# Batched attention on one core: a third bank for exponentiated scores, short uses in the ring of maxima banks, and outputs that keep the heads on partitions

## The reference, cut to what matters

```python
x = x + attn_a(_layernorm(x), w_qkv, w_proj)          # causal, 16 heads of 16, T = 512
x = x + ffn(_layernorm(x), ...)                       # full attention, then a routed expert layer
x = x + attn_b(_layernorm(x), ...)                    # short attention with relative positions
x = x + ffn(_layernorm(x), ...)                       # the same weights as the second layer

# attn_a, per head                                    # ffn's attention, per head
a = where(causal, q @ k.T * 0.25, -inf)               # scores = q @ k.T * 0.25
a = clip(a, -100, 100)                                # probs = softmax(scores)
e = exp(a - max(a))                                   # attn = probs @ v, then @ Wo + bo
p = e / (sum(e) + 1e-6) + 1e-8
out = (p / sum(p)) @ v, then @ w_proj.T
```

## Time and profile before

| | |
|---|---|
| runs of the kernel before | 2593.06, 2582.32, 2595.44 us; median 2593.06 us |
| the profiled execution | 2579.53 us, span of its instructions 2577.8 us, mean granted PE clock 0.977 |
| PE busy | 2418.6 us, 94% |
| DVE busy | 1831.9 us, 71% |
| ACT busy | 1438.2 us, 56% |
| POOL busy | 1351.5 us, 52% |
| DMA | 305.88 MB, mean 119 GB/s |

### The profile page before, as it was taken

How to read it: one execution, slowest core, us unless ns; L and a number is a source line. 1 busy time by engine, 2 the same in 40 slices (tenths; PEclk the granted TensorE clock), 3 DMA queues, 4 the chain that set the end, 5 groups by cost and what they waited for, 6 DMA issues and landing times. The chain is left out here.

```text
span 2577.8 us, 45874 instructions
## 1 busy us (share of the span) xinstructions
PE 2418.6 (94%) x14724; PEld 1393.9 (54%) x14724; DVE 1831.9 (71%) x3685; ACT 1438.2 (56%) x2991; POOL 1351.5 (52%) x1358
## 2 busy tenths in 40 slices
PE   6999999999999999989999699988999999989998
PEld 3455555554444444349899366653344434349997
DVE  5999999999778888854333558867778888845333
ACT  3666666666777777753333232214777777653332
POOL 5356666563234554444655579843334454435655
PEclk8999999999999999999999799988999999999999
DMA  5333333333434444324665200015434444335654
GB/s 161 101 105 107 105 102 108 112 105 96 120 112 124 133 129 125 98 93 161 213 201 179 72 1 17 17 58 138 118 109 129 129 130 122 85 118 176 202 194 141
DMA packets 249936, 305.88 MB, mean 119 GB/s; under 512 B 28034, under 2 KB 224865, under 8 KB 249700
## 3 DMA queue, kind: packets, MB, share of 16 engines
q1 hardware_dynamic: 238164, 275.37, 35.8%
q0 software_dynamic: 10176, 26.27, 2.9%
q10 hardware_dynamic: 1360, 1.31, 0.2%
HBM read 210.32 MB, written 92.84 MB: 118 GB/s over the span
## 5 line engine op out<-in xcount | busy, mean ns | idle before, releaser
L783 DVE TENSOR_REDUCE neg_max_af<-sc_af 128x1 f32<-128x512 f32 (+3 forms) x864 | 551.0, 664 | 105.2 <-PE sc_af L489 101.2
L704 ACT ACTIVATE prob_af<-sct_af 128x512 f32<-128x512 f32 (+1 forms) x864 | 484.1, 582 | 234.9 <-PE sct_af L512 231.3
L783 DVE TENSOR_REDUCE neg_max_f<-sc_f 128x1 f32<-128x512 f32 x512 | 334.6, 685 | 93.0 <-PE sc_f L489 90.8
L704 ACT ACTIVATE prob_f<-sct_f 128x512 f32<-128x512 f32 x512 | 290.6, 598 | 127.5 <-PE sct_f L512 126.1
L512 PE MATMUL sct_af<-stack_q_af,stack_k_af 99*128 99x512 bf16 (+3 forms) x1024 | 320.1, 343 | 7.9 <-ACT prob_af L704 7.1
L489 PE MATMUL sc_af<-stack_k_af,stack_q_af 96*128 96x512 bf16 (+3 forms) x1024 | 320.0, 342 | 4.1 <-DVE neg_max_af L783 4.0
L1620 PE MATMUL y_ps_e<-w_r,hT_e 128*128 x1120 | 255.4, 381 | 5.7 <-issue 4.0
L812 DVE SCALAR_TENSOR_TENSOR prob_af<-prob_af,w_r 128x512 f32<-128x512 f32 (+2 forms) x224 | 233.2, 1049 | 21.7 <-ACT prob_af L704 21.5
L1807 DVE TENSOR_TENSOR y_e<-y_ps_e,b_e 128x256 f32<-128x256 f32 x70 | 29.7, 425 | 298.3 <-PE y_ps_e L1620 296.5
L540 PE MATMUL out_af<-prob_af,v_aug_af 128*32 128x512 f32 (+3 forms) x2048 | 231.9, 525 | 8.7 <-DVE prob_af L812 7.8
L1620 PEld LDWEIGHTS y_ps_e<-w_r,hT_e 128*128 128x128 f32 x1120 | 207.2, 190 | 35.3 <-issue 9.4
(11 more groups left out here) (383 smaller groups left out, 4650.0 us busy)
## 6 DMA issues: line engine op xcount, KB each, us to landing
w_r<-in_f_W_dram SPq DMA_DIRECT2D x66, 1024.0 KB, 5.1
stack_k_af<-k_parts_d SPq DMA_DIRECT2D x64, 384.0 KB, 4.3
k_parts_d<-parts_af SPq DMA_DIRECT2D x187, 128.0 KB
q_parts_d<-parts_af SPq DMA_DIRECT2D x96, 128.0 KB
stack_q_af<-q_parts_d SPq DMA_DIRECT2D x64, 192.0 KB, 2.9
stack_k_f<-k_parts_d SPq DMA_DIRECT2D x32, 384.0 KB, 4.2
w_next<-in_f_W_dram SPq DMA_DIRECT2D x12, 1024.0 KB, 4.9
k_parts_d<-parts_f SPq DMA_DIRECT2D x91, 128.0 KB
```

The costliest lines, as they stand in the source:

```text
L704: nc.scalar.activation(dst, src.rearrange("p (h q) -> p h q", h=len(heads)), ACT.Exp).then_inc(S.exp_done, 1)
L783: nc.vector.tensor_reduce(M.neg_max[:, qt, heads[0]:heads[-1] + 1], src, AX.X, ALU.max, negate=True).then_inc(S.max_done, 1)
```

## The change

- PSUM: three `sct` banks (`exp` may lag three units), three `sc` banks, one `out`, one `gen`. The light uses now take turns with the scores in the ring of the three `sc` banks (`place`, `used_before`); heavy uses have `gen`.
- Outputs keep the heads on partitions. SP moves the 16 rows of each head from `o_sb` straight into `attT`, which is double now, and the row sums into `sums` (`move_out`, 5 DMAs a group). For each half of the heads (a chunk, c = 0 or 1) DVE works out the weights on a [128, 32] tile (`weigh`: 4 instructions causal, 1 otherwise), SP stores them to DRAM (`store_weights`) and reads them back repeated over each head's 16 rows (`spread_weights`), and POOL multiplies `attT` by them in place (`scale_out`: 3 instructions causal, 1 otherwise). The transposes `out` and `attT`, `normalise`, `add_floor` and ACT's copy of `attT` go.
- The old way stays for the second chunk of the last two units of each call that ends in ffn units (`by_pe`: n = 14, 15, 22, 23).
- The three bf16 parts of the maxima are laid out so that one transpose of [128, 48] does for four of [128, 12]; `max_sb` is [48, 128] instead of [12, 512].
- The sum of all v comes as one column per chunk (two matmuls of 1 column) instead of 256 columns on all partitions.
- Some pairs of semaphores are merged.

```diff
-    closing = [("out", last, NG - 1), ("attT", last, 0), ("attT", last, 1), ("y", last, 0), ("y", last, 1)]
-    for at, use in enumerate(opening):
-        place(use, (at + 1) % 2)
+    closing = [("out", last, NG - 1), ("attT", last, 1), ("y", last, 0), ("y", last, 1)]
...
+    def bank(use):
+        uses, at = place_of[use]
+        return M.sc[at % len(M.sc)] if uses is ring else M.gen
+
+    def used_before(use):
+        uses, at = place_of[use]
+        back = len(M.sc) if uses is ring else 1
+        return uses[at - back] if at >= back else None
     for n in range(first, end):
         for s in range(SLOTS_N):
-            if light_at(n, s):
-                place(light_at(n, s), 1)
-            if heavy_at(n, s) and s % 2 == 0:
-                place(heavy_at(n, s), 0)
+            g, kt = divmod(s, KT)
+            light, heavy = light_at(n, s), heavy_at(n, s)
+            for i in range(4):
+                place_scores(*group(n, g + 2), kt, i)
+                if light and i == (2 if kt == KT - 1 else 0):
+                    place(light, ring)
+            if heavy and s % 2 == 0:
+                place(heavy, gen_uses)
...
+            def move_out(n, g):
+                if not exists(n) or by_pe(n, g // 2):
+                    return
+                c, h = divmod(g, 2)
+                sp.wait_ge(S.o_sb, NG * n + g + 1)
+                if n > 1:
+                    sp.wait_ge(S.y_ps, 2 * (n - 1))
+                if exists(n - 1) and by_pe(n - 1, 1):
+                    sp.wait_ge(S.attT_ps, pe_chunks(n - 1))
+                sp.dma_start(M.sums[64 * h:64 * h + 64, :], M.o_sb[HD:P:32, :]).then_inc(S.moved, 16)
+                for i in range(4):
+                    o = 64 * h + HD * i
+                    sp.dma_start(M.attT[n % 2][o:o + HD, c, :], M.o_sb[32 * i:32 * i + HD, :]).then_inc(S.moved, 16)
+
+            def store_weights(n, c):
...
+                sp.wait_ge(S.weighed, chunks(n, c))
+                sp.dma_start(M.weights_d[n % NB][0, hs, :], M.weights[:, 0, :]).then_inc(S.weights_stored, 16)
+                if causal(n):
+                    sp.dma_start(M.weights_d[n % NB][1, hs, :], M.weights[:, 1, :]).then_inc(S.weights_stored, 16)
+
+            def spread_weights(n, c):
...
+                sp.wait_ge(S.weights_stored, 16 * spreads(n, c))
+                sp.wait_ge(S.moved, 80 * moved(n, 2 * c + 1))
...
+                for at in range(2 if causal(n) else 1):
+                    sp.dma_start(M.spread[:, at, :], M.weights_d[n % NB][at, hs, :].unsqueeze(1).to_broadcast([8, HD, T])).then_inc(S.weights_spread, 16)
...
-                    for t in range(KT):
-                        last = nc.tensor.transpose(Gb[0:12, t * P:t * P + P], M.max_parts[:, t, :, :].rearrange("p a h -> p (a h)"), C.ident_bf[:, :])
+                    last = nc.tensor.transpose(bank(use)[:, :].bitcast(BF16)[0:12 * KT, 0:P], M.max_parts[:, :, :, :].rearrange("p a h t -> p (a h t)"),
+                                               C.ident_bf[:, :])
...
                 u = exp_unit(n, g, kt, i)
-                if u >= 2:
-                    pe.wait_ge(S.exp_done, u - 1)
-                bank = M.sct[u % 2]
+                if u >= 3:
+                    pe.wait_ge(S.exp_done, u - 2)
+                bank = M.sct[u % 3]
...
             def read_out(n, g):
                 act.wait_ge(S.pv_done, pv_count(n, g, KT - 1))
-                if n > 0 or g > 0:
-                    act.wait_ge(S.out_ps, NG * n + g)
+                pn, pg = group(n, g - 1)
+                if exists(pn) and by_pe(pn, pg // 2):
+                    act.wait_ge(S.out_ps, outs(pn, pg))
+                elif exists(pn):
+                    act.wait_ge(S.moved, 80 * moved(pn, pg))
...
+            def weigh(n, c):
...
+                dve.wait_ge(S.moved, 80 * moved(n, 2 * c + 1))
...
+                    nc.vector.tensor_scalar(M.e8[:, :], M.sums[:, :], 1e-6, 1e-8, ALU.add, ALU.mult).then_inc(S.norm_step, 1)
...
+                    nc.vector.tensor_tensor(M.weights[:, 1, :], M.e8[:, :], M.weights[:, 0, :], ALU.mult).then_inc(S.weighed, 1)
...
                         if kt == 2:
                             normalise(pn, pg)
+                        if kt == 3 and pg % 2 == 1:
+                            weigh(pn, pg // 2)
...
+            def scale_out(n, c):
...
+                pool.wait_ge(S.weights_spread, 16 * spreads(n, c))
+                out = M.attT[n % 2][:, c, :]
+                if causal(n):
...
+                    nc.gpsimd.tensor_tensor(out, out, M.spread[:, 0, :], ALU.mult).then_inc(S.floor_v, 1)
+                    nc.gpsimd.tensor_scalar(M.spread[:, 1, :], M.spread[:, 1, :], M.v_all[:, n % 2, c:c + 1], None, ALU.mult).then_inc(S.floor_v, 1)
...
+                    nc.gpsimd.tensor_tensor(out, out, M.spread[:, 1, :], ALU.add).then_inc(S.attT_ready, 1)
```

301 lines of the change are left out of this document (168 added, 133 removed).

## The result

The changed kernel takes 2659.43 us (median of 4 runs, 2643.36 to 2674.43), the kernel before, measured beside it, 2590.18: the ratio is 1.0265, with a 95% interval of 1.0237 to 1.0294. It is slower by 2.6%; the forecast was 2533 us, faster by 2.3%. The profiled span is 2641.6 us against 2577.8, the mean granted PE clock 0.954 against 0.977.

The account below looks back on a forecast made before the run. PE was taken as the bound, nearly full in causal and full in ffn units; -73 (PE's list) + 8 (ring) + 13 (maxima rows) - 7 (third bank) - 1 (tail) = -60 us from 2593: 2533 us, range 2500 to 2572.

Parts of the forecast that it names:

- all five cases: PE's list decides (0.58), costs hide too (0.15), DVE holds causal units (0.12), transfers run late (0.07), no effect (0.08).
- the slow one: SP's list: maxima rows of every causal group leave late, 31 floor rows each stand 2.9 us more; 2610 us, chance 0.07.
- the first case: PE's shorter list in the attention units decides the time: 2533 us, bounds 2510 to 2562, chance 0.58.
- What leaves PE: Attention units: fewer transposes for out, attT and maxima save PE 3.26 us a unit, 73 us over 24 units.
- The port that DVE and POOL share: Causal units: POOL's longer floor work could cost DVE 16 us at most; none booked, DVE not alone the bound.
- The maxima rows: Causal units, group 2: rows leave 2.3 us late, PE stands 1.8 us in 7 units; +13 us, between 0 and 22.
- group 0: Causal units, SP's list: no delay booked, since for three of four groups SP has nothing to wait for.
- The ring: Slot 8 of 16 ffn units: a score waits for ACT's copy of xnT, 0.5 us each; +8 us, bounds 0 and 24.
- the third bank: PE runs one exponential further ahead, shortening waits for clipped probabilities in causal units; -7 us, at most 36.

Follow-up runs that it names:

- e10: e8 with the banks of the kernel before (two for exponentiated scores, one general each for heavy and light uses): 2552.57 us, 0.9857 of the kernel before.
- e14: e13 with SP's read-back of the weights also cut to 16 of 512 columns, leaving out work: 2572.14 us, 0.9919 of the kernel before.
- e2: Changed kernel with the maxima rows of groups 2 and 0 ahead of the weights' read-back in SP's list: 2618.88 us, 1.0091 of the kernel before.
- e7: e2 with DVE's split of the maxima behind the clip made of six single-input reductions: 2575.72 us, 0.9959 of the kernel before.
- e8: e6 and e7 together: 2563.73 us, 0.9916 of the kernel before.
- e11: Control: the kernel before with only the split of the maxima as six single-input reductions: 2589.62 us, 1.0015 of the kernel before.
- e5: The kernel before with the change of banks alone (three for exponentiated scores, light uses in the ring): 2813.10 us, 1.0861 of the kernel before.
- e13: Changed kernel with POOL's scale_out on only 16 of 512 columns, leaving out work: 2628.66 us, 1.0183 of the kernel before.
- e15: e10 with POOL's scale_out on only 16 of 512 columns, leaving out work: 2538.00 us, 0.9804 of the kernel before.
- e6: e2 with POOL's scale_out(n-1,0) between the second and third split and scale_out(n-1,1) behind scale_y: 2596.79 us, 1.0034 of the kernel before.
- e9: e8 with DVE's weigh(n-1,1) moved from slot 3 to the end of slot 4, its store behind the maxima rows: 2566.69 us, 0.9920 of the kernel before.
- e12: e10 with DVE's weigh(n-1,1) in slot 5 behind both clips, its store behind the maxima rows: 2570.28 us, 0.9927 of the kernel before.
- e1: Changed kernel with POOL's scale_out(n-1,0) in causal units moved from ahead of the splits to right before scale_out(n-1,1): 2781.82 us, 1.0697 of the kernel before.

## Why the prediction was wrong

The measured 2659 us lies outside all five cases, above the slow one as well (2610, chance 0.07). The bounds of the first case, 2510 to 2562, do not quite follow from its terms either (2512 to 2565, with 0 to 7 us gained); nothing hangs on that.

**What leaves PE: right.** With their stalls gone (e10) the ffn stages took 498.2 and 433.9 us against 518.7 and 452.6: 39.2 us over 15 units, 2.6 us a unit, where 3.26 was booked for 11 of them and 1.97 for the other 4, 2.9 on average. In the causal units only e14, which leaves out work, is below the kernel before, by 2.0 a unit; every complete version is above it.

**The port that DVE and POOL share: the step that failed.** The prediction booked none of it, "since DVE is not alone the bound", put its upper bound at 16 us, the growth of POOL's time, looked for it in the causal units alone and said of DVE in the ffn units that "it does not matter". These reasons were of the wrong kind. A held instruction costs by what waits for it, and DVE's split of the maxima is a chain of small ones with PE's next transpose behind it: 0.2 us of work became 1.1 or 2.0 us. And it need not be new POOL work that holds it; `scale_out` moved the old splits and `scale_y` there. What it measured: taking away the hold at that chain alone gave 1.32% or 34 us by the ratios (e2 to e7, 43 by the medians), with POOL's order 1.75% or 45 us (e2 to e8), and nothing in the kernel before, where that chain was held less and PE waited little for it (e11). By the stages it stood where the prediction had not looked: from e2 to e7 the ffn stages fell by 16.7 and 27.7 us, the causal units by 0.7, since there the clips, held as well, came next. The prediction had read that the same subtraction takes 1732 ns in one stage and 1157 in the other, and had asked only what this costs POOL.

**The maxima rows: the right mechanism, a third to a half of its size.** Booked were 13 us, at most 22, for group 2. Moving the rows ahead gave 1.74% or 45 us (41 by the medians; 28 in the causal stage of the profiles, 10 of them lost clock). The issue was 2.3 us late, as forecast, and the stall of group 2 itself 1.39 us in the unit shown, below the 1.8 booked, because PE came late as well. What the sum lacked was group 0, the landing and the clock behind the stalls. Of the landing I took 2.9 us "as the shorter rows of DMAs show", for a transfer that has 512 KB just ahead of it, and it was 5.65 to the floor row. For the same reason group 0, which I had cleared because SP has nothing to wait for there, stalled 2.47 us. The slow rival, a landing more at every floor row, was drawn too wide: two of four groups waited.

**The ring and the third bank.** +8 and -7 were booked; together they are +11 to +15 (e8 to e10), inside the bounds of the ring's term alone. The wait named for the ring, a score behind ACT's copy of `xnT`, is there (2.2 us in 300 in e8, where 0.5 a unit was booked), and so is the third bank's gain (1.4 us of waits for exponentials where e10 has 6.0); no run has one without the other, so neither is priced alone. That the ring is at all payable hangs on the outputs (e5).

**The clock, which stood in no term.** Lost clock over the span went from 58 to 121 us. It fell behind two stalls of 2 us in the stretch shown and behind the single one of 3.08 us in e8, so a stall is not only its own length. In e14, whose longest stalls are 1.8 us, it is 5.1 us in the causal units against e13's 54.6; in e2, e7, e8 and e10, where the floor rows are in time too but stalls of 2.1 to 3.1 us are left, it is 22 to 26.

**The sum.** The span grew by 63.8 us where 60 less were forecast. By the ratios, rows in time give 45 us of that back, the free split and POOL's new order 45, the old banks 15. That ends at 0.9857, 37 us below the kernel before, against the forecast 60. In the attention stages of the profiles e10 has the 39 us that the ffn units were to give and a loss of 9 in the causal ones, where about 23 were forecast as a gain. The three stages of e15 add 13: POOL's work on `attT` costs that even where it is well placed. The 7.8 and 6.4 us of the two stages with the experts and the third layer can't be laid to the change: their code, but for unit 16 and some merged semaphores, is the same in all kernels, and yet they took 699.8 and 287.7 us in e11 and 715.3 and 289.2 in e6, where that first stage lost most clock (56.3 us).

What stays open: why the last stall of a causal unit, the clips beside POOL's third split, is 3.0 to 3.1 us in e8, e10 and e15, while the kernel before has the same two neighbours and 0.5 us, and e14, where the two clips took 3.36 us together, 1.8. The weights' 1.2 us ahead of it are not the whole reason (e9, e12). That `pv` stall is still in the best version.

## What to carry to other kernels

Before adding work to POOL, list which small instructions of DVE have two SBUF inputs or are copies, and which of them the critical engine waits for; then look where POOL's queue will stand at that time, its old work too. A chain of single-input reductions is immune and costs 0.2 us a step. A small transfer that someone waits for goes ahead of large ones in the queue, even if these leave only 1 us earlier, and its landing is priced behind them, not from the median of a calm stretch. And a stall is priced with the clock behind it. A control that changes nothing says little until the trace shows whether there was anything to free.

## What was unexpected of the hardware

- A cast of 128x16 took 0.17 to 0.19 us free, and 1.02 to 2.05 us beside POOL's 128x512 and 128x1024 operations, ending within 0.05 us of them; a reduction of that size never more than 0.198, in any run.
- Two clips of 128x1024 (one takes 1.21 us when free) and a POOL subtraction of 1.16 us took turns: the clips showed 3.34 us together and the subtraction 2.01.
- Behind two stalls of 2.1 us, 3 us apart, the granted clock was 0.58 over 3 us, and the same behind a single one of 3.08 us; with stalls of up to 10.1 us at the floor rows (e1) the mean of 300 us was 0.81.
- A row transfer issued 1.3 us behind two of 256 KB let PE go on 5.65 us after its issue, behind two of 8 KB 2.70 us.
